# First layer of a four-layer graph network: score pieces worked in sides of four, with output products of 16 key tiles together

## The reference

```python
q, k, v = jnp.split(x @ Wqkv + bqkv, 3, axis=-1)           # heads of 64
scores = jnp.einsum('hnd,hmd->hnm', qh, kh) * SCALE
scores = scores + graph_bias * adj_matrix[None, :, :]
scores = jnp.where(adj_matrix[None, :, :] == 0, -1e9, scores)
attn = jax.nn.softmax(scores, axis=-1)
out = jnp.einsum('hnm,hmd->hnd', attn, vh)
out = out.transpose(1, 0, 2).reshape(n, d) @ Wout + bout
```

## Time and profile before

| | |
|---|---|
| median of three runs | 3090.18 us (3089.05 to 3092.65) |
| span of the profiled execution | 3085.8 us, 4.4 us under that median |
| first transposition of the first layer's main loop to its end | about 98 to 1668 us |
| PE, DVE, ACT, POOL busy | 2998.1, 2100.8, 1895.1, 873.0 us |
| TensorE clock granted in the first layer | 1.00 |

### The profile page before, as it was taken

One profiled execution on the slowest core, in us unless ns is written; L12 is line 12 of the kernel. 1 busy time (PEld: TensorE's weight loads), 2 busy tenths in 40 slices (PEclk: granted clock), 3 DMA queues, 4 the chain that ended last, 5 costly groups with the idle time before them and its releaser, 6 DMA issues.

```text
span 3085.8 us, 45339 instructions
## 1 busy us (share of the span) xinstructions
PE 2998.1 (97%) x16612; PEld 2168.6 (70%) x16612; DVE 2100.8 (68%) x3607; ACT 1895.1 (61%) x2705; POOL 873.0 (28%) x514
## 2 busy tenths in 40 slices
PE   8999999999999999999998899999999999999998
PEld 5677777777777777777776555555558888788887
DVE  6677777777777777777775987777626455565564
ACT  4677777777777777777775677777654333433332
POOL 2134422343134422343130355455511011000000
PEclk9999999999999999999999999999999999999999
DMA  6699899989898998899877233333159988989882
GB/s 187 140 171 187 183 186 165 184 186 198 167 173 182 187 188 170 177 185 198 168 130 280 78 137 127 135 145 123 48 148 217 213 203 200 219 218 208 205 196 59
DMA packets 721788, 530.49 MB, mean 172 GB/s; under 512 B 565536, under 2 KB 601888, under 8 KB 705184
## 3 DMA queue, kind: packets, MB, share of 16 engines
q1 hardware_dynamic: 678384, 441.07, 61.3%
q10 hardware_dynamic: 36288, 66.08, 11.6%
q0 software_dynamic: 6896, 20.45, 2.3%
HBM read 439.36 MB, written 88.08 MB: 171 GB/s over the span
## 4 chain that ended last, share of the span: by engine, by line
PE 82%; DVE 10%; issue 3%; ACT 2%; DMA 1%; POOL 1%; SPq 0%; DVEq 0%; POOLq 0%; ACTq 0%
PE at_score L529 15%; PE at_o L554 12%; PE gl_four L1379 12%; PE at_turn L541 11%; PE gl_quad L1432 7%; PE gl_quad L1434 7%; PE gl_quad L1433 7%; DVE at_probs L781 4%; PE gl_quad L1362 3%; PE at_mixed L563 2%; PE gl_four L1405 2%; DVE at_bias L747 2%; PE at_mixed L512 1%; DMA gl_first_weights<-in_adj 1%; DVE at_probs L801 1%
## 5 line engine op out<-in xcount | busy, mean ns | idle before, releaser
L781 DVE CUSTOM_DVE_ANT_0 at_probs<-at_score,at_bias 128x1024 f32<-128x1024 f32 x509 | 621.5, 1221 | 391.1 <-PE at_score L529 388.0
L668 ACT ACTIVATE at_pT<-at_turn 128x1024 f32<-128x1024 f32 x512 | 521.2, 1019 | 276.9 <-PE at_turn L541 275.2
L529 PE MATMUL at_score<-at_kT,at_q 128*128 128x512 f32 x2036 | 611.7, 422 | 34.2 <-DVE at_maxima L781 34.2
L659 ACT ACTIVATE at_probs<-at_probs,at_minus_max 128x1024 f32<-128x1024 f32 x512 | 586.0, 1144 | 64.7 <-DVE at_minus_max L786 63.9
L455 POOL TENSOR_SCALAR at_masked<-at_bias 128x512 bf16<-128x512 f32 x240 | 482.7, 2031 | 444.7 <-DMA at_bias<-in_adj 342.6
L554 PE MATMUL at_o<-at_pT,at_values 128*64 128x256 f32 x4096 | 498.3, 385 | 0.0
L541 PE MATMUL at_turn<-all_ident,at_probs 128*128 128x128 f32 x4096 | 489.0, 272 | 0.0
L541 PEld LDWEIGHTS at_turn<-all_ident,at_probs 128*128 128x128 f32 x4096 | 462.3, 140 | 35.4 <-issue 1.5
L1379 PE MATMUL gl_four<-gl_early,gl_first_wh 128*128 128x512 f32 x1024 | 460.8, 593 | 6.0 <-ACT gl_early L1500 6.0
L529 PEld LDWEIGHTS at_score<-at_kT,at_q 128*128 128x128 f32 x2036 | 352.1, 189 | 152.2 <-DVE at_maxima L781 82.1
L1525 ACT ACTIVATE gl_split<-gl_units 128x1024 fp32r<-128x1024 f32 x256 | 263.8, 1055 | 278.5 <-PE gl_quad L1434 278.5
(11 more groups left out here) (130 smaller groups left out, 2970.3 us busy)
## 6 DMA issues: line engine op xcount, KB each, us to landing
gl_units<-adjT SPq DMA_DIRECT2D x512, 256.0 KB, 7.6
at_bias<-in_adj SPq DMA_DIRECT2D x128, 512.0 KB, 6.5
at_probs<-in_adj SPq DMA_DIRECT2D x256, 256.0 KB, 5.4
adjT<-at_probs SPq DMA_DIRECT2D x1024, 64.0 KB, 4.4
gl_first_weights<-in_adj SPq DMA_DIRECT2D x32, 2048.0 KB, 8.3
at_values<-v_heads ACTq DMA_DIRECT2D x252, 256.0 KB, 4.8
gl_early<-x SPq DMA_DIRECT2D x160, 128.0 KB, 2.6
x<-gl_early POOLq DMA_DIRECT2D x64, 128.0 KB, 2.7
```

Source lines behind the costliest of these rows:

```text
L529: last = pe.matmul(place[:, at], q[:, q_place(h), part, t * P:(t + 1) * P], kT[:, h, col:col + BANK], start=part == 0, stop=part == 1)
L659: act.activation(part, part, ACT.Exp, bias=minus_max[:, k, t:t + 1], scale=1.0, accum_out=sums[:, k, t, pp:pp + 1]).then_inc(prob_ready, 1)
L668: act.activation(pT[:, j % PT_SLOTS, :], turn_bank[j % 2][:], ACT.Copy).then_inc(pT_ready, 1)
L781: dve.tensor_tensor_reduce(out=ring[:, place_in_ring(u, pp), t, :], in0=place[:], in1=bias[:, t, at], scale=SCALE, scalar=LOWEST, op0=ALU. ...
```

## The change

The beat loop becomes a loop over sides, halves of a unit with four beats each (eight sides per chunk, numbered 0 to 7; r = 0 to 3 within a side). On PE a side is S, T, S, T T, S, T, S and then both quarters of output products. The three PSUM places are shared by scores and transposes: steps 0 to 7 of each side take them in rotation, so every step takes the place that was used three steps before and waits for that one's reader. ACT copies between and after, with one exponential between its first two copies and three at the side's end. DVE's small tasks move to slots (side, r); its blocks come in groups of up to three (`BLOCKS_AT`), still 17 per chunk. POOL makes the masks of six of eight pieces; those of pieces 3 and 6 (`WIDE`) DVE makes itself, a whole piece at a time, in the memory of `xs`, which SP therefore loads a second time in each chunk. After `make_q`, `keep_q` and `finish_q` now follow in the same side instead of in the next unit; for head 2 of the first chunk they are in the prologue.

```diff
-    MAKE_BIAS = {17: 0, 18: 1, 20: 2, 21: 3, 23: 4, 24: 5, 25: 6, 26: 7}
+    MAKE_BIAS = {(4, 1): 0, (4, 3): 1, (5, 1): 2, (5, 2): 3, (5, 3): 4, (6, 0): 5, (6, 1): 6, (6, 2): 7}
...
-    BLOCK_BEATS = (0, 2, 4, 6, 8, 10, 12, 14, 15, 17, 19, 22, 24, 27, 28, 30, 31)
+    SIDE = BEATS // 2
+    SIDES = CHUNK_BEATS // SIDE
+    SCORE_STEP = (0, 2, 5, 7)
+    TURN_STEP = (1, 3, 4, 6)
+    SIDE_STEPS = 2 * SIDE
+    BLOCKS_AT = {(0, 1): 1, (0, 3): 2, (1, 3): 3, (2, 1): 1, (2, 3): 2, (3, 1): 1, (3, 3): 1, (6, 3): 2, (7, 1): 1, (7, 3): 3}
+    CHUNK_BLOCKS = sum(BLOCKS_AT.values())
+    WIDE = (3, 6)
+    NARROW = tuple(i for i in range(BEATS) if i not in WIDE)
...
+        wide_mask = xs[:].rearrange("p t d -> p (t d)").bitcast(BF16)
...
+        def blocks_in(c, side, r):
+
+            before = sum(n for slot, n in BLOCKS_AT.items() if slot < (side, r))
+            first = CHUNK_BLOCKS * c + before
+            return [b for b in range(first, first + BLOCKS_AT.get((side, r), 0)) if b < BLOCKS]
...
+        pool_of_places = (turn_bank[1], turn_bank[0], score_bank)
+
+        def score_place(side, r):
+
+            return pool_of_places[(SIDE_STEPS * side + SCORE_STEP[r]) % 3]
+
+        def turn_place(side, r):
+
+            return pool_of_places[(SIDE_STEPS * side + TURN_STEP[r]) % 3]
...
+                        if h == 1 and half == 0 and r == 2:
+                            sync.wait_ge(acc_start, CT * (c + 1))
+                            sync.dma_start(xs[:], x_tiles[:, bass.ds((c + 1) * CT, CT), :]).then_inc(x_loaded, 16)
+                        if h == H - 1 and half == 1 and r == 1:
+                            wait(sync, wide_used, len(WIDE) * (c + 1))
+                            sync.dma_start(xs[:], x_tiles[:, bass.ds((c + 1) * CT, CT), :]).then_inc(x_loaded, 16)
+                        if BIAS_LOAD <= at < BIAS_LOAD + BEATS:
+                            i = at - BIAS_LOAD
+                            sync.wait_ge(score_read, CHUNK_BEATS * c + (H - 1) * BEATS + i + 1)
+                            load_bias(c + 1, i)
...
-                    for i in range(BEATS):
+                    for i in NARROW:
...
+                if turned_out:
+                    pe.wait_ge(pT_ready, turned_out)
+                else:
+                    wait(pe, score_read, BEATS * u + i - unread)
...
+            def turn_probs(s, j, place, place_read, place_copied):
+
+                wait(pe, score_read, min(place_read, BEATS * UNITS))
+                wait(pe, pT_ready, place_copied)
...
+                        last = pe.transpose(place[:, a * CN + t * P:a * CN + (t + 1) * P],
...
-                for h, j, at in beats():
...
-                    far = unit_after(c, h, (j + AHEAD) // BEATS)
-                    if j % 2:
-                        turn_probs(s, j)
-                    if not (last and h + (j + AHEAD) // BEATS >= H):
-                        make_scores(*far, (j + AHEAD) % BEATS)
-                    if j % 2 == 0:
-                        turn_probs(s, j)
-                    elif j > 1:
-                        aggregate(c, h, j // 2 - 1)
-                    elif has_before:
-                        aggregate(*before, TWINS - 1)
...
+                    scores(0, 1)
+                    turn_probs(s, j0, turn_place(G, 0), 0, beat)
+                    scores(1, 1)
+                    turn_probs(s, j0 + 1, turn_place(G, 1), beat + AHEAD + 1, 0)
+                    if half == 1 and h == 1 and not last:
+                        pe.wait_ge(acc_ready, s)
+                        turn_x(c + 1)
+                    turn_probs(s, j0 + 2, turn_place(G, 2), 0, beat + 1)
+                    scores(2, 0)
+                    turn_probs(s, j0 + 3, turn_place(G, 3), 0, beat + 2)
+                    scores(3, 0, beat + 3)
...
                         project(s - 1, before[1])
-                    if j == 5 and h == 1 and not last:
-                        pe.wait_ge(acc_ready, s)
-                        turn_x(c + 1)
-                    if j == 7 and h % 2 and not (last and h + 3 >= H):
+                    if half == 1 and h % 2 and not (last and h + 3 >= H):
                         wait(pe, acc_ready, s)
                         make_q(*unit_after(c, h, 3))
+                    aggregate(c, h, 2 * half)
+                    aggregate(c, h, 2 * half + 1)
...
+                    if half == 0 and has_before:
                         keep_oT(s - 1)
...
+                    for q in (2, 3) if half == 0 else (0, 1):
+                        if has_before if half == 0 else not (last and h == H - 1):
+                            act.wait_ge(aggregated, TWINS * (s + half - 1) + q + 1)
+                            at_q = slice(q * (NT // TWINS), (q + 1) * (NT // TWINS))
+                            act.dma_start(values[:, q, :, :], v_heads[(h + half) % H][:, at_q, :])\
+                               .then_inc(value_loaded[q], 16)
+                    keep_pT(s, j0, turn_place(G, 0), is_first(c, h))
+                    exps(0)
+                    keep_pT(s, j0 + 1, turn_place(G, 1), is_first(c, h))
+                    if half == 1 and h == 1 and not last:
...
+                    keep_pT(s, j0 + 2, turn_place(G, 2), False)
+                    keep_pT(s, j0 + 3, turn_place(G, 3), False)
+                    if half == 1 and h % 2 and not (last and h + 3 >= H):
+                        keep_q(*unit_after(c, h, 3))
+                    for r in range(1, SIDE):
+                        exps(r)
...
+                dve.wait_ge(x_turned, c + 1)
+                dve.wait_ge(adj_loaded[i], 16 * (c + 1))
+                wait(dve, wide_used, n)
+                dve.tensor_scalar(wide_mask, part, 0.0, MASKED / SCALE, ALU.is_equal, ALU.mult).then_inc(wide_masked, 1)
+                dve.wait_ge(wide_masked, n + 1)
+                dve.scalar_tensor_tensor(out=part, in0=part, scalar=gain[:, 0:1], in1=wide_mask,
+                                         op0=ALU.mult, op1=ALU.add).then_inc(wide_used, 1)
...
-                    if not (last and h + (j + AHEAD) // BEATS >= H):
-                        read_scores(*unit_after(c, h, (j + AHEAD) // BEATS), (j + AHEAD) % BEATS)
...
-                    if at in MAKE_BIAS and not last:
-                        make_bias(c + 1, MAKE_BIAS[at])
-                    b = block_in(c, at)
-                    if b is not None:
-                        turn_block(b)
...
+                    for r in range(SIDE):
+                        j = j0 + r + AHEAD
+                        if not (last and h + j // BEATS >= H):
+                            read_scores(*unit_after(c, h, j // BEATS), j % BEATS, score_place(G, r))
+                        if r == 1:
+                            if half == 1:
+                                invert_sums(s, h % 2)
+                            if side == 1 and has_before and c:
+                                dve.wait_ge(acc_ready, s)
+                                ln.statistics(dve, acc, c - 1)
+                            if side == 2:
+                                start_acc(c)
+                        if r == 3:
+                            if half == 0 and has_before:
+                                add_step(s - 1, before[1], before[1] % 2, before[0])
+                            if side == 1 and c:
+                                ln.normalise(dve, acc, c - 1)
+                            if half == 1 and h % 2 and not (last and h + 3 >= H):
+                                for e in range(2):
+                                    finish_q(*unit_after(c, h, 3), e)
+                        if (side, r) in MAKE_BIAS and not last:
+                            i = MAKE_BIAS[side, r]
+                            if i in WIDE:
+                                make_wide_bias(c + 1, i)
+                            else:
+                                make_bias(c + 1, i)
+                        for b in blocks_in(c, side, r):
+                            turn_block(b)
+                        if last:
+                            early(dve, SIDE * side + r)
```

137 lines of the change are left out of this document (66 added, 71 removed).

## The result

| | before | changed |
|---|---|---|
| median (runs) | 3089.61 us (4) | 3183.55 us (4; 3181.8 to 3193.9) |
| ratio | | 1.031, interval 1.0293 to 1.0328 |
| span of the profiled execution | 3085.8 us | 3180.1 us |
| period of a chunk in the trace | 99.2 us | 105.3 us |
| the same, kernel f1 below | | 93.7 us, median 3006.6 us |

The change is 94 us slower; 3037 was forecast.

The account below looks back on a forecast made before the run. PE, busy 97% of the span, was taken as the bound. 41 us from its blocks plus 12 us from fewer waits (2.0 instead of 2.8 us a chunk) made 53 us less: 3037 us, range 3012 to 3075.

Parts of the forecast that it names:

- TensorE's own blocks: On PE, regrouped output products, score blocks and transposes save 0.33 us per side over 125 sides: 41 us.
- A chunk without waits: PE's work per chunk in the kernel before, four projections and two q included: 96.3 of 99.15 us.
- P: The projection on PE, moved between score block and output products: taken as no extra cost, 0 to 10 us lost possible.
- the waits of a side fit: In PE's plan for a side, each shared PSUM place is free before it is wanted, with 0.04 to 0.45 us spare.
- Rival C: No block saving arrives: every side waits 0.3 us for ACT's copies; 3075 to 3090 us, chance 7%.
- Side 6 and the other waits without blocks: PE's waits per chunk: 0.9 us in side 6, 0.3 in side 3, 0.3 for DVE's full sides 5 to 7.
- The blocks: Grouped blocks arrive late at DVE after three at once: 0.5 us of waits a chunk, at most two of 1 us.
- rival B: SP's bursts of stores make blocks and bias late for DVE: 5 us of PE waits a chunk, 3082 us, chance 11%.
- my own table of places: The times each shared PSUM place is free and wanted within a side, such as free at 4.32, wanted at 4.50 us.
- Rival A: DVE's wide mask and bias pieces stall behind GpSimd's masks in sides 5 and 6: 3151 us, chance 8%.

Follow-up runs that it names:

- f1: The changed kernel with blocks one at a time and next-chunk bias pieces made earlier, slot (6, 0) left empty; 3006.6 us, ratio 0.9734 to the kernel before.
- a_spread: The changed kernel with its 17 blocks a chunk one at a time, at the old kernel's beats, nothing else changed; 3039.3 us, ratio 0.9839 to the kernel before.
- b_narrow: The changed kernel with all eight masks made by GpSimd again (no wide pieces), bursts of blocks kept; 3244.1 us, ratio 1.050 to the kernel before.

## Why the prediction was wrong, by its own steps

**TensorE's own blocks: right.** 41 us were forecast from 0.33 per side. The measured blocks are A of 32 in 3.60, S in 1.01 between two T, T of 8 in 0.79 to 0.80. A chunk without waits came to 96.3 - 8 x 0.33 = 93.7 us; f1's is 93.7. P cost nothing in its new place, as taken: S before it is followed after 1.01, P takes 0.96 and A 3.60, so beside an S before A of 1.10 it costs 0.87, as between A and S before:

```profile
864.41 1.17 PE L579 MATMUL at_turn<-at_kT,at_q 128*128 128x512 f32 x4
865.42 1.02 PE L614 MATMUL at_mixed<-at_wo,at_oT 128*128 128x256 f32 x4
```

**Whether the waits of a side fit: right.** Five bullets said 0.04 to 0.45 us to spare; f1 and the calm sides show that nothing is lost there. Rival C (ScalarE) never came: between 250 and 1550 us ACT's copies end no wait of PE.

**Side 6 and the other waits without blocks: right in sum.** 1.5 of the 2.0 us of waits a chunk had nothing to do with blocks: 0.9 at slot (6, 0), 0.3 in side 3, 0.3 for the full sides. c, the changed kernel without blocks, has a chunk of 95.0, 1.3 above 93.7, and the changed kernel's waits before score blocks are 1.1 us a chunk. All of them stand in side 6; ScalarE's copy in side 3 ended none. In a_spread they are larger, since DVE also turns a block (747.51, 0.70 us) between the bias piece of slot (6, 0) and the next reading.

**The blocks: the step that failed.** The text read: "the next ones arrive 2.15 + 5.4 us or more later, up to 2 us after DVE comes to them. They stand at r = 1 and 3, where 2 us are mostly spare ... I take 0.5 us", and the upper end was two waits of 1 us. The term was 0.5 us a chunk; measured, the blocks cost 105.3 - 95.0 = 10.3 us a chunk (changed kernel and c). In the chunk followed above two waits of PE, 3.2 and 4.4 us, and the half clock behind them came from it.

Four things were wrong or left out. First, the chain is longer than one store and one load. SP stores the first block of a burst, loads, stores the second, loads, stores the third, loads: the last of the three pays all of it. With the forecast's own 2.15 and 5.4 us, and 0.6 for issuing each load before, an estimate for the burst of (1, 3) gives 3 x 2.15 + 2 x 0.6 + 5.4 = 13.1 us from 857.14, so 870.2. DVE came for that block at 871.1, and without its wait of 3.3 us at (2, 1) it would have come at 867.9: over 2 us too early already. I wrote this chain for rival B in words but gave it 1 us. Second, SP's issue time is no constant. The three stores took 10.4 us instead of 6.5, and the loads were usable after 7.0 and 6.1 us. The 2.15 of the earlier trace rows is a short one. This is the longest for a block in the kernel before, where blocks come one at a time:

```profile
657.72 6.64 SPq L369 DMA_DIRECT2D adjT<-at_probs  x4
```

Between 250 and 1550 us the longest in the changed kernel is 6.19. So long issues are not made by bursts alone, though over 5.2 us there are 4 in that stretch before and 11 in the changed kernel. Blocks that are spread out have the time for them. Third, r = 3 of a side has no spare at all when its block comes last before the next r = 0, the slot where my own table of places left 0.2 us. Fourth, the load of x stands on the same queue, and PE waited 1.8 us a chunk for it; the forecast counted it only as bytes.

**Rival B** named the place and the mechanism, with 5 us of waits a chunk and 11%; it asked too little of them. Its 3082 is 8 us won; the measured chunk is 11.6 us above one without waits. No case held that. **Rival A**, on the right side of zero, was the wrong mechanism; a_spread, which keeps the wide pieces, b_narrow and the rows of L827 and L829 exclude it.

**The clock** was in no term. By PE's busy time above it cost about 48 us in the loop, some 3 us a chunk.

## What to carry to other kernels

When small tasks with a transfer behind them are regrouped, follow the whole chain (store issues, landing, load issues, landing) from one to the one that reuses its place, at the slowest issue time in the trace, not at that of one calm row. Then ask which slot of the waiting engine has spare time, since an in-order engine hands a late transfer to everything queued behind it. Here one constant with the slots spread out evenly turned 94 us lost into 50 won, and starting the bias pieces earlier, so that none stands in the tight slot (6, 0), another 33.

## What was not expected of the hardware

Waits of TensorE in the middle of a steady loop were often, not always, followed by a stretch at half clock, with eight transposes busy 1.97 us instead of 1.04: after one of 1.89 us the clock was 0.72, after one of 3.23 it was 1.00. All of it together kept PE busy about 48 us longer. Four stores of 64 KB in runs of 128 bytes held SyncE's queue for 2.1 us in one place and for up to 6.6 in another, in the kernel before too. A VectorE mask of 1024 columns took 0.69 to 1.05 us and its bias instruction 1.28 to 1.51 beside GpSimd's masks of 1.91 to 2.46: no instruction of either was held up for the length of the other's.
